# Conv 2 of a graph network on one core: ScalarE makes the residual one pair ahead instead of two

## The reference

```
h   = relu(layernorm(x))
r   = h                                          # the residual
h   = gelu(layernorm(gcn(h, W1) + b1) * g1 + be1)        # conv 1
h   = layernorm(gcn(h, W2) + b2) * g2 + be2              # conv 2
x2  = x + gelu(h + r)
h   = relu(layernorm(x2))
out = x2 + gcn(h, W3) + b3                               # conv 3
```

## Time and profile before

| | |
|---|---|
| median of 3 runs | 3271.37 us |
| profiled execution, its own time | 3272.66 us |
| span of its trace | 3270.8 us |
| busy share PE / DVE / ACT / POOL | 89% / 78% / 63% / 63% |
| conv 2, about | 1320 to 2390 us of the span |

### The profile page before, as it was taken

How to read it: one execution, slowest core, us unless ns; L and a number is a source line. 1 busy time by engine, 2 the same in 40 slices (tenths; PEclk the granted TensorE clock), 3 DMA queues, 4 the chain that set the end, 5 groups by cost and what they waited for, 6 DMA issues and landing times. The chain is left out here.

```text
span 3270.8 us, 60605 instructions
## 1 busy us (share of the span) xinstructions
PE 2904.5 (89%) x16427; PEld 2433.2 (74%) x16427; DVE 2548.5 (78%) x6373; ACT 2053.4 (63%) x3083; POOL 2062.6 (63%) x1615
## 2 busy tenths in 40 slices
PE   8233369999999999799999999999969999999999
PEld 2122258888888888688888888888758888888888
DVE  9899968888888888699999999999934454444544
ACT  0266556777767776689888989999933333333333
POOL 0122257777777775688888888888755555555553
PEclk9999999999999999899999999999979999999999
DMA  3399987888888786799999999999789999999996
GB/s 133 149 382 418 411 237 217 214 216 217 214 219 215 213 215 168 241 317 326 320 315 314 324 318 316 316 322 319 263 240 287 286 290 289 286 289 286 288 287 209
DMA packets 304977, 890.18 MB, mean 272 GB/s; under 512 B 67209, under 2 KB 67707, under 8 KB 304922
## 3 DMA queue, kind: packets, MB, share of 16 engines
q1 hardware_dynamic: 189082, 681.53, 60.0%
q0 software_dynamic: 115840, 208.01, 26.8%
HBM read 652.74 MB, written 307.71 MB: 294 GB/s over the span
## 5 line engine op out<-in xcount | busy, mean ns | idle before, releaser
L840 POOL DMA_INDIRECT gathered<-H,idx x826 | 1155.5, 1399 | 514.9 <-issue 237.7
L1228 PE MATMUL out<-Whi,ahi 128*128 128x512 f32 x2832 | 778.9, 397 | 39.8 <-ACT out L923 38.5
L914 ACT ACTIVATE ahi<-agg 128x1024 fp32r<-128x1024 f32 x354 | 360.8, 1019 | 642.6 <-PE agg L1219 642.6
L1228 PE MATMUL out<-Wlo,ahi 128*128 128x512 f32 x2832 | 761.6, 391 | 0.0
L1228 PE MATMUL out<-Whi,alo 128*128 128x512 f32 x2832 | 739.4, 390 | 0.1
L1228 PEld LDWEIGHTS out<-Wlo,ahi 128*128 128x128 f32 x2832 | 533.4, 188 | 116.0
L1228 PEld LDWEIGHTS out<-Whi,ahi 128*128 128x128 f32 x2832 | 509.9, 189 | 146.0 <-ACT out L923 50.9
L1228 PEld LDWEIGHTS out<-Whi,alo 128*128 128x128 f32 x2832 | 531.5, 188 | 110.9 <-DVE alo L1039 0.5
L1031 DVE TENSOR_TENSOR vlo<-gathered,vhi 128x512 fp32r<-128x512 f32 x354 | 243.0, 686 | 319.4 <-ACT vhi L908 319.4
L1039 DVE TENSOR_TENSOR alo<-agg,ahi 128x1024 fp32r<-128x1024 f32 x354 | 429.5, 1213 | 57.6 <-ACT ahi L914 56.9
L923 ACT ACTIVATE out<-vec,sqrt_deg 128x512 f32<-128x512 f32 x708 | 458.0, 681 | 16.4 <-PEq L750 9.8
(11 more groups left out here) (162 smaller groups left out, 3730.1 us busy)
## 6 DMA issues: line engine op xcount, KB each, us to landing
gathered<-H SPq DMA_DIRECT2D x351, 512.0 KB, 6.1
H<-ho SPq DMA_DIRECT2D x250, 512.0 KB, 4.3
x<-in_x_dram SPq DMA_DIRECT2D x165, 512.0 KB, 8.1
X<-x SPq DMA_DIRECT2D x117, 512.0 KB
x<-X SPq DMA_DIRECT2D x117, 512.0 KB, 7.4
out_dram<-conv SPq DMA_DIRECT2D x117, 512.0 KB
H<-x SPq DMA_DIRECT2D x48, 512.0 KB, 9.8
gathered<-H,idx POOLq DMA_INDIRECT x826, 5.4
```

The costliest lines, as they stand in the source:

```text
L840: pool.indirect_dma_start(rows, None, H[q][0:end, :], bass.IndirectOffsetOnAxis(ap=idx[p.slot(4)][:, c:c + 1], axis=0), bounds_check=end - ...
L914: nc.scalar.activation(Ahi[p.slot(2)][:, :], Agg[p.slot(2)][:, :], ACT.Copy)\
L1228: m = nc.tensor.matmul(Out[2 * p.slot(2) + j][:, :], a[p.slot(2)][:, c:c + P], w[q][:, f, :], start=False, stop=stop and f == KD - 1, skip ...
```

## The change

In conv 2's ScalarE body relu_x(p+2) becomes relu_x(p+1), in the same place. Ahead of the first body ScalarE makes R(0) alone. Nothing else changes: SyncE still loads x(p+2) in body p, there are still two buffers of R and four of x, and GpSimd still takes R(p) in its body p.

```diff
@@ -985,8 +985,7 @@
                             if second:
                                 high(p.after(1))
                                 over_high(p.after(2))
-                                for k in range(2):
-                                    relu_x(k, p.after(k))
+                                relu_x(0, p)
                                 over_high(p.after(3))
                                 seed(1, p.after(1))
                         if second:
@@ -1000,8 +999,8 @@
                                 seed(of(known, 2), p.after(2))
                             if has(known, -2):
                                 relu_x2(of(known, -2), p.after(-2))
-                            if has(known, 2):
-                                relu_x(of(known, 2), p.after(2))
+                            if has(known, 1):
+                                relu_x(of(known, 1), p.after(1))
                             if has(known, 4):
                                 over_high(p.after(4))
                             return
```

## The result

| | before | after |
|---|---|---|
| median | 3271.22 us (4 runs) | 3622.69 us (4 runs, 3622.12 to 3623.09) |
| span of the profiled execution | 3270.8 us | 3620.2 us |
| conv 2, pace per pair | 8.80 us | 11.82 us |

The ratio is 1.1076, interval 1.1057 to 1.1095: 10.8% slower. The forecast was 3569, in a range of 3522 to 3640. The pace is worked out as in the earlier trace rows, from the first and last start of y's halves: (2725.8 - 0.7 - 1342.3)/117 = 11.82. 3.02 us a pair times 117 is 353 us, so the whole of the +351 is in the pace of conv 2. The edit removed a line, so what was L1085 is L1084 from here on, and so for the lines behind it.

A forecast was written before the change was run, and what follows sets the result against it. The load loop of x was taken to set conv 2's 8.80 us a pair; a one-pair loop over GpSimd, links summing to 11.1, taken as 11.4, would replace it: +297 us, so 3569, range 3522 to 3640.

The forecast's parts named there:

- the one-pair ring over GpSimd: Conv 2: residual, addition, gather, power, y, gelu, next residual close within one pair, 11.1 to 11.75 us; chance 0.88.
- residual to additions: ScalarE to GpSimd in conv 2: first half of the residual 0.81 us plus a handoff of 0.15.
- a slower gather: GpSimd's gather beside x2_sum could exceed its 1.03 us; +0.35 a pair, 40 us, allowed in the range.
- The collision of x2_sum and the additions: VectorE's x2_sum meets GpSimd's first addition and waits for its end; the second addition is delayed by 0 or 0.65 us.
- the lower end: Second addition goes on at once, so x2_sum costs the loop nothing: 11.1 us a pair, 3534 us.
- the upper: x2_sum's half slips between the additions, making all behind 0.65 us later: 11.75 us a pair, 3609 us.
- the middle: Conv 2's pace taken as 11.4 us a pair, as no row showed whether x2_sum or the second addition goes first.
- a gap between the additions of 1.24 or 1.9: On GpSimd, 1.24 us between the two additions would mean 11.1 us a pair, 1.9 would mean 11.75.
- the step from GpSimd to VectorE: Handoff from the end of GpSimd's power to VectorE's x2_scale, taken as 0.03 us.
- squares and high: ScalarE's work after x2's mean, 2.3 us, ends at 10.9, before gelu may start at 11.1 or later, so hidden.
- Each pair starts slow: TensorE in conv 2 restarts each pair at the 1.2 GHz level and recovers, costing 1.7 us, hidden.
- The worth of the load wait: Removing ScalarE's wait for the load of x could gain at most about 46 us, down to TensorE's 8.4 a pair.

The follow-up runs named there:

- the best complete version: Kernel before, with the load of x issued three pairs ahead and x2_var_eps moved to the head of VectorE's body: 3233.57 us, ratio 0.9880.

## Why the prediction was right

**The direction and the mechanism.** The likeliest case named the one-pair ring over GpSimd, and the rows after show it link by link. It was confirmed from three sides: leaving GpSimd's addition out gave 3220, taking the gather or power out gave 3501 and 3456, and the load alone, moved, does nothing to the kernel after (3622) and gains on the kernel before (3240).

**The terms of the sum.**

| link | forecast | measured, the turn above |
|---|---|---|
| gelu to residual | 3.59 | 3.60 |
| residual to additions | 0.96 | 0.89 |
| additions to gather | 2.68 to 3.33 | 3.14 |
| gather to power | 1.07 (up to 1.57) | 1.33 |
| power | 1.04 | 1.04 |
| power to x2_scale | 0.03 | 0.25 |
| x2_scale to end of y, to gelu | 1.74 | 1.73 |
| sum | 11.1; 11.4 taken; 11.75 | 11.98 |

The pace forecast was 11.1 to 11.75, and both what it came to over the whole of conv 2 (11.82) and this turn (11.98) lie above. The time still fell in the range because the range had room for a slower gather (+0.35 a pair, 40 us). Its upper end was added up wrongly on the way: 3609 + 40 is 3649, not 3640. The 54 us by which 3569 was low are three mis-sized terms. The collision of x2_sum and the additions: the lower end said that the second addition goes on, the upper that x2_sum slips in at 0.65. x2_sum does slip in, and it costs 0.46; the middle stood for 0.3, which was an average of two cases and not a reading. The sign that was to tell them apart, a gap between the additions of 1.24 or 1.9, would have misled: the trace starts the second addition 1.26 after the first and books the wait as part of its duration. The gather beside x2_sum: 1.30 instead of 1.03, which was kept for the range only. And the step from GpSimd to VectorE, which was read where conv 2 drains and is 0.17 to 0.25 in the two turns looked at. In the other direction, residual to additions was put 0.07 too high.

The additions and gather in the kernel after, 1400 to 2690 us, columns as in the earlier trace rows:

```profile
L876 POOL TENSOR_TENSOR r<-r,vec x216: 1277/1516/1751, 1405.3 to 2679.6; 128x512 f32<-128x512 f32 x108
```

```profile
L840 POOL DMA_INDIRECT gathered<-H,idx x108: 1023/1302/1312, 1408.4 to 2681.5; - x108
```

The first addition takes about 1.28, the second up to 1.75, of which 0.46 is waiting for x2_sum's first half. The last starts of L876 give the steady ring: (2679.6 - 1.5 - 1405.3)/107 = 11.90 us.

**What was said of the others.** x2_sum longer than 0.68 (1.14 and 1.76) and L1111 back at 0.14, as written. TensorE was busy 463.8 us of the 600 from 1500 to 2100, 77% against about 75%, at a mean granted clock of 0.93. GpSimd's wait for ScalarE is 3.7 us, more than the 2 to 3 foreseen, since the ring is longer. High ends at 1922.50, 1.29 us before gelu starts: squares and high are hidden, as forecast.

**TensorE's clock.** Two turns of the ring, as stretches (columns as in the earlier trace rows):

```profile
1899.94:1911.81 11.87, 10.04 (x48) 8.32 (x48) 9.68 (x23) 8.05 (x13) 7.55 (x7) 0.86 0.70 238
1911.81:1923.79 11.98, 8.41 (x48) 7.19 (x48) 9.65 (x23) 8.06 (x13) 7.66 (x7) 1.00 0.70 236
```

In one turn the granted clock was 0.86, with part of the work at the 1.2 GHz level, and TensorE took 10.04 us for what takes 8.41 in the next: 1.6 more, against 1.7 forecast. The turn with the dip is no longer than the other: the dip is covered. In the first TensorE had waited 3.44 us for sv before its products, in the second 1.83. The length of the pause alone doesn't tell: in the kernel before, a pause of 1.57 us was followed by slow products. "Each pair starts slow", as the rule of the Trainium skill ("TensorE: Matmul & The Clock Gate", Part 1) was applied in the prediction, was too strong: not each did.

**The worth of the load wait** was put at 46 us. The whole computation with an early load gave 28, then 39; without the addition 50. Part of what is missing is VectorE's waiting for GpSimd inside x2_var_eps, which the page of the profile books as busy time: taking that away gave 7 us (3240 to 3234). The prediction also divided TensorE's busy time by the pairs and took 8.4 us a pair as reachable; the best complete version came to 8.49, with TensorE busy all but 1.5 of 600 us. Why it needs 0.1 us a pair more there than without the addition (8.37) stays open.

## What to carry to other kernels

Shortening a lead to give a transfer time moves the slack from the transfer to whoever consumes the result: before doing it, write down the ring that the shorter lead closes and add up its starts; if it goes over another engine's in-order queue, everything ahead on that queue is in the sum. Here the load could be given its period by issuing it past a store that blocked its queue, and little came in (0.15 us a pair in x2_var_eps). And when work on GpSimd is moved in time, look at every VectorE instruction that it lands on, the tiny ones too.

## What the runs showed of the hardware that I had not expected

- GpSimd and VectorE take turns instruction by instruction: x2_sum's first half got in between two additions queued back to back, at 0.46 us for GpSimd and 1.5 us in all for VectorE (1.14 + 1.76 instead of 0.68 twice). With more of them in a row it was 3.54 us for two additions of 2.53.
- A tensor_scalar on 128x2 with two constants waited for GpSimd's addition (0.50 us), one on 128x1 with a column as its scalar didn't (0.21).
- GpSimd's power on 128x4 took 1.49 us instead of 1.04 when it began right behind an addition beside x2_sum, and the issue of a gather 1.30 to 1.53 instead of 1.03 beside x2_sum or y. With the additions kept clear of x2_sum, power's median was 1.23.
